# Cross-attention: division of the values' product in place of the probabilities, and one expert unit in another place

## The chip, the cores and the metric

The kernel runs on one core of a Trainium2 chip. Its engines work through queues of their own and meet through semaphores: TensorE (PE; its weight loads are shown as PEld), VectorE (DVE), ScalarE (ACT), GpSimd (POOL) and SyncE (SP), which issues most of the DMAs. The metric is device time in microseconds (us) of one launch, as the median of several runs; lower is better. Times inside the kernel come from one execution that the hardware profiler took.

## The reference, cut to what matters

A decoder block on 128 sequences of 64 tokens of 128 numbers: agent attention, cross-attention to a context of 64 tokens, and 16 experts of which each token uses two, each behind a layer norm and added to the input. The change is in the cross-attention, 16 heads of 8 numbers:

```python
Q = _split_heads(query @ Wq.T)
K = _split_heads(key @ Wk.T)
V = _split_heads(value @ Wv.T)
scores = jnp.einsum('bhqd,bhkd->bhqk', Q, K) / jnp.sqrt(jnp.float32(D_K))
causal = jnp.where(jnp.tril(jnp.ones((S, S), dtype=bool)), 0.0, NEG_INF).astype(scores.dtype)
scores = scores + causal[None, None, :, :]
attn = jax.nn.softmax(scores, axis=-1)
heads = jnp.einsum('bhqk,bhkd->bhqd', attn, V)
concat = heads.transpose(0, 2, 1, 3).reshape(B, S, D)
out = concat @ Wo.T
```

## The kernel before

The 128 sequences are worked on in eight groups of 16 (1024 tokens, eight tiles of 128). Every engine's program calls `both(e, g)` (run, L290): the experts of group e lie beside the two attentions of group g = e + 1. The first call has no e, the last no g, so there are seven full passes. The order of the work on each engine is written out by hand in its own `both`, and the engines wait for each other by semaphores.

Cross-attention of a group goes in four units u of four sequences, each with four planes q. On TensorE `scores(g, u)` (L587) adds the causal mask (L598) and the products of queries and keys (L606) in four PSUM banks of the ring "att", one bank a plane; the next unit's scores take the same banks and wait until they are read. On VectorE `maxima` (L1211) finds the largest score of each row; for planes 1 to 3 it subtracts it at once (L1222) and ScalarE takes the exponential of the whole plane (L935), for plane 0 ScalarE does both in eight short instructions, one a head (L930). `inverses` (L1225) sums the exponentials on VectorE (L1233) and takes the reciprocal (L1235); GpSimd multiplies 14 of the 16 planes of a group by it (L426), VectorE the other two (`normalise_x`, L1247). Then TensorE transposes the plane (`turn`, L624), ScalarE copies it out (`PT_moved`), `values` (L627) multiplies it with V, `project` (L640) with the output weights, and VectorE adds the result (`add_x`, L1239). For `values` the weights are V itself, spread over 32 columns with zeros (tile Vb), and the probabilities are moved, 128 columns at a time; for `project` the output weights were spread with zeros in a tile woM, by 16 DMAs at the start (L325). `values` of unit u runs two units behind its scores; the last two units' values and projections of group e fall in the next pass, among the first steps of group g: transposes of context and input, the values of the context (`values_of`, L654), the layer norm `norm`/`apply` (L1058, L1074), the pooled queries (L1286) and the products `moments` (L669).

An expert unit (`unit`, L520) is six products of 512 columns (`up`), one that spreads the routing weight (`weight`), and the down products of the unit before (`down_to`). VectorE's `hidden` (L1146) multiplies its parts, `result` (L1175) adds the sum of nine units. There are 18 units, 0 to 17, for each group. Unit 17 stands ahead of scores(0), its down products right behind them.

## Time and profile before

| | before |
|---|---|
| runs, us | 1148.42, 1150.33, 1150.6; median 1150.33 |
| span of the profiled execution, us | 1150.6 |
| busy: TensorE, its weight loads | 975.8 us (85%), 767.2 us (67%) |
| busy: VectorE, ScalarE, GpSimd | 788.8 us (69%), 577.3 us (50%), 227.7 us (20%) |
| chain that ended last, by engine | PE 62%, DVE 21%, ACT 10%, POOL 3% |

The profiled execution's span is that of its run, 1150.6 us; the runs differ by 2.2 us. Busy shares are means over stages with different limits, so the rows below are from single stages. The granted clock is a share of TensorE's full speed: 1.00 is 2.4 GHz, 0.50 is 1.2 GHz; a mean between them is a mixture. A row's name of a tile is the program's: banks are PSUM, M holds the transposed planes (pT), KQ and PXUT the planes themselves, Vb and woM the spread values and weights.

### The profile page before, as it was taken

The page shows a single profiled execution, that of the slowest core. Times are in us where ns is not written, and L with a number is a line of the kernel's source. Part 1 is how long each engine was busy: PE and PEld are TensorE (multiplying, and loading weights), DVE is VectorE, ACT ScalarE, POOL GpSimd, SP SyncE. Part 2 cuts the span into 40 slices and gives each one's busy share as a digit, 9 for nine tenths or more (in the row PEclk, how much of TensorE's full clock was granted, in tenths as well). Part 3 has the DMA queues.
Part 4 walks back from the last instruction along what each step waited for, and adds up shares of the span by engine and source line. Part 5 has one row for each costly group of instructions (what it writes and reads, how often), then busy time and mean ns, then how long its engine had stood idle before and what let it go on. Part 6 is the DMA issues. An engine that isn't in the chain of part 4 may idle for free.

```text
span 1150.6 us, 22137 instructions
## 1 busy us (share of the span) xinstructions
PE 975.8 (85%) x9069; PEld 767.2 (67%) x9069; DVE 788.8 (69%) x1841; ACT 577.3 (50%) x1148; POOL 227.7 (20%) x220
## 2 busy tenths in 40 slices
PE   6656899969998799978999699987999689987687
PEld 5553688737785587846886487855787477864566
DVE  3256866687866967678667878678666867669444
ACT  4434755367534665357553565346652575445322
POOL 6001410035000520024100440014200341004100
PEclk9886999979998899979999799989999799997789
DMA  5300010000100010000100010000100000000000
GB/s 146 80 1 1 2 38 1 11 10 2 38 10 10 2 38 1 11 10 2 37 11 1 11 31 8 10 11 2 38 1 10 11 2 1 10 11 1 1 1 19
DMA packets 28902, 18.36 MB, mean 16 GB/s; under 512 B 7649, under 2 KB 27394, under 8 KB 28802
## 3 DMA queue, kind: packets, MB, share of 16 engines
q1 hardware_dynamic: 26914, 12.48, 4.2%
q0 software_dynamic: 1280, 4.20, 1.2%
q8 instruction: 72, 1.18, 0.4%
q10 hardware_dynamic: 608, 0.27, 0.1%
q14 instruction: 28, 0.23, 0.1%
HBM read 12.62 MB, written 4.19 MB: 15 GB/s over the span
## 4 chain that ended last, share of the span: by engine, by line
PE 62%; DVE 21%; ACT 10%; POOL 3%; issue 3%; SPq 1%; DMA 0%; DVEq 0%; POOLq 0%
PE banks L510 7%; PE banks L674 5%; PE banks L491 5%; PE banks L493 5%; PE banks L492 5%; PE banks L606 4%; PE banks L624 4%; ACT M L867 3%; PE banks L648 3%; DVE PXUT L1222 3%; DVE mx L1221 3%; PE banks L769 3%; PE banks L541 2%; DVE sil L1166 2%; PE banks L598 2%
## 5 line engine op out<-in xcount | busy, mean ns | idle before, releaser
L874 ACT ACTIVATE sil<-banks,b 128x512 f32<-128x512 f32 x144 | 99.5, 691 | 199.6 <-PE banks L493 197.2
L867 ACT COPY M<-banks 128x512 f32<-128x512 f32 x208 | 122.9, 609 | 90.3 <-PE banks L624 70.2
L1166 DVE SCALAR_TENSOR_TENSOR sil<-banks,b,sil 128x512 f32<-128x512 f32 x128 | 95.8, 749 | 93.6 <-ACT sil L874 91.8
L510 PEld LDWEIGHTS banks<-w,hT 128*128 128x128 f32 x1152 | 151.5, 194 | 12.5 <-issue 7.2
L510 PE MATMUL banks<-w,hT 128*128 128x128 f32 x1152 | 154.5, 277 | 1.4 <-DVE hT L1173 1.4
L389 POOL DMA_DIRECT2D out_x<-xn x16 | 12.9, 809 | 534.3 <-DVE xn L1179 534.3
L426 POOL TENSOR_TENSOR PXUT<-PXUT,rx 128x512 f32<-128x512 f32 x80 | 87.2, 1117 | 101.7 <-DVE rx L1235 101.7
L1173 DVE TENSOR_TENSOR hT<-sil,banks 128x512 f32<-128x512 f32 x128 | 87.9, 687 | 25.1 <-PE banks L500 21.3
L624 PE MATMUL banks<-ident,PXUT 128*128 128x128 f32 x384 | 61.9, 301 | 31.7 <-ACT M L867 28.2
L598 PE MATMUL banks<-maskb,pick 32*64 32x512 bf16 x512 | 46.4, 506 | 46.6 <-ACT PXUT L930 28.2
L674 PEld LDWEIGHTS banks<-pooled,A 128*128 128x128 f32 x512 | 66.1, 207 | 19.9 <-DVE pooled L1286 18.6
L624 PEld LDWEIGHTS banks<-ident,PXUT 128*128 128x128 f32 x384 | 44.1, 150 | 52.6 <-ACT M L867 40.0
L674 PE MATMUL banks<-pooled,A 128*128 128x128 f32 x512 | 68.9, 293 | 12.0 <-DVE pooled L1286 12.0
L491 PE MATMUL banks<-xnT3l,w1h 128*128 128x512 f32 x144 | 75.1, 522 | 0.3 <-ACT sil L874 0.3
L491 PE MATMUL banks<-xnT3l,w3h 128*128 128x512 f32 x144 | 61.4, 427 | 11.1 <-DVE sil L1166 10.3
L1221 DVE TENSOR_REDUCE mx<-banks 128x8 f32<-128x512 f32 x96 | 65.3, 681 | 0.0
L867 ACT COPY PXUT<-banks 128x512 f32<-128x512 f32 x64 | 36.0, 588 | 54.6 <-PE banks L581 30.7
L606 PE MATMUL banks<-KQ 32*64 32x256 f32 x1024 | 60.9, 547 | 0.0
L493 PE MATMUL banks<-xnT3h,w1h 128*128 128x512 f32 x144 | 59.3, 412 | 0.0
L493 PE MATMUL banks<-xnT3h,w3h 128*128 128x512 f32 x144 | 59.2, 411 | 0.0
L1233 DVE TENSOR_REDUCE lx<-PXUT 128x8 f32<-128x512 f32 x96 | 59.2, 658 | 0.0
L492 PE MATMUL banks<-xnT3h,w1l 128*128 128x512 f32 x144 | 59.2, 411 | 0.0
(199 smaller groups left out, 2067.2 us busy)
## 6 DMA issues: line engine op xcount, KB each, us to landing
xin<-in_x SPq DMA_DIRECT2D x8, 512.0 KB, 4.1
cin<-in_ctx SPq DMA_DIRECT2D x8, 512.0 KB, 5.3
out_x<-xn POOLq DMA_DIRECT2D x16, 256.0 KB, 2.8
KQ<-in_L_attn_Wqkv SPq DMA_DIRECT2D x3, 512.0 KB, 5.3
KQ<-in_L_ffn_We SPq DMA_DIRECT2D x2, 512.0 KB, 4.6
KQ<-in_L_attn_Wo SPq DMA_DIRECT2D x1, 512.0 KB, 8.0
w<-in_L_ffn_We SPq DMA_DIRECT2D x1, 512.0 KB
woM<-xwT SPq DMA_DIRECT2D x16, 8.0 KB, 1.8
```

Source lines behind the costliest of these rows:

```text
L491: mm(ps(name)[:], wh[:, 2 * p:2 * p + 2, :], xl, start=True, stop=False)
L492: mm(ps(name)[:], wl[:, 2 * p:2 * p + 2, :], xh, start=False, stop=False)
L493: mm(ps(name)[:], wh[:, 2 * p:2 * p + 2, :], xh, start=False, stop=True).then_inc(fulled(name), 1)
L510: mm(ps(name)[:, P * t:P * t + P], hT[:, k % 2, P * t:P * t + P], w2[:, pair[k], :], start=(n == 0 and t == 0), stop=False, skip_group_che ...
L606: last = mm(ps(name)[64 * r:64 * r + 64, 256 * t:256 * t + 256], Qx[rr, S * b:S * b + S], Kx[rr, :, S * b:S * b + S], start=False, stop=Tr ...
L624: last = turn_over(ps(name)[:, P * j:P * j + P], src[:, P * j:P * j + P], ident[:])
L674: last = mm(ps(f"M_{n}")[:, P * k:P * k + P], A[:, 4 * (n % 4) + k, :], pooled[:], start=True, stop=True)
L867: cp(dst, ps(name)[:] if src is None else src).then_inc(ready, 1)
L874: nc.scalar.activation(sil[:, k % 2, :], ps(f"H1_{k}")[:], ACT.Silu, bias=b1[:, pair[k]:pair[k] + 1]).then_inc(sil_ready, 1)
L1166: V.scalar_tensor_tensor(sil[:, k % 2, :], ps(f"H3_{k}")[:], b3[:, p:p + 1], sil[:, k % 2, :], ALU.add, ALU.mult).then_inc(hid_ready, 1)
L1173: V.tensor_tensor(hT[:, k % 2, :], sil[:, k % 2, :], ps(f"C_{k}")[:], ALU.mult).then_inc(hT_ready, 1)
L1221: link(V.tensor_reduce(mx[:, q], sv, AX, ALU.max), g)
```

## The change

V gets a column of ones for each head (tile Vx in place of Vb). `values` now takes the transposed exponentials as weights and moves Vx, 18 columns for two heads at a time; what comes out has the tokens as rows, and beside each head's eight numbers the sum of its exponentials. The sums, reciprocals and multiplications of the planes go, and so do GpSimd's part of the cross-attention, woM and its 16 DMAs with the waits for them. `normalise_O` on VectorE divides the product instead. Then TensorE transposes it (`turn_O`), ScalarE copies it, and `project` multiplies it with the output weights as they are; the transposed product and the projection share one PSUM bank in turn. Plane 0 is subtracted on VectorE like the other three. Unit 17 now stands behind scores(0), its down products behind scores(1); the transposes and products that make the queries stand one unit earlier, and values_of(g, 3) ahead of the input's transposes.

```diff
-             "yx": ([f"Yx_{u}" for u in range(UX)], 1)}
+             "yx": ([f"{kind}_{u}" for u in range(UX) for kind in ("OT", "Yx")], 1)}
...
-            sp.wait_ge(consts, 3)
-            sp.wait_ge(setup_cp, 2)
-            for s in range(2):
-                for b in range(2):
-                    for gq in range(4):
-                        sp.dma_start(woM[32 * gq + 16 * b:32 * gq + 16 * b + 16, s, b, :],
-                                     xwT[32 * gq + 16 * s:32 * gq + 16 * s + 16, 3, :]).then_inc(spread_wo, 16)
...
-            nc.gpsimd.memset(woM[:], 0.0)
-            nc.gpsimd.memset(Vb[:], 0.0)
+            step(nc.gpsimd.memset(Vx[:], 0.0))
+            for r in range(2):
+                step(nc.gpsimd.memset(Vx[64 * r:64 * r + 64, :, :, (XC + 1) * r + XC:(XC + 1) * r + XC + 1], 1.0))
...
-                        nc.gpsimd.tensor_tensor(p, p, rx[:, u % 2, q].unsqueeze(2).to_broadcast([P, HALF, S]),
-                                                ALU.mult).then_inc(pn_ready, 1)
...
-                for j in range(4):
-                    for q in range(XQ):
-                        rr = slice(32 * q, 32 * q + 32)
-                        last = mm(ps(name)[rr, P * j:P * j + P],
-                                  Vb[:, 2 * u + j // 2, 2 * q + j % 2, :, :].rearrange("p a c -> p (a c)"),
-                                  pT[:, (XQ * u + q) % PT, j, :], start=True, stop=True, tile_position=(0, 32 * q))
+                w = 2 * (XC + 1)
+                for t in range(2):
+                    for j in range(XH // 2):
+                        for r in range(2):
+                            o0 = w * (XH // 2) * t + w * j
+                            last = mm(ps(name)[64 * r:64 * r + 64, o0:o0 + w],
+                                      pT[:, (XQ * u + j // 2) % PT, 2 * t + j % 2, 64 * r:64 * r + 64],
+                                      Vx[:, 4 * u + 2 * t + r, j, :], start=True, stop=True)
...
+            def turn_O(g, u):
...
+                pe.wait_ge(On_ready, UX * g + u + 1)
                 for t in range(2):
+                    last = turn_over(ps(name)[:, P * t:P * t + P], On[:, u % 2, t, :], ident[:])
...
+                for t in range(2):
+                    last = mm(ps(name)[:, P * t:P * t + P], OnT[:, u % 2, t, :], xwT[:, 3, :], start=True, stop=True)
...
-                unit(e, 17)
...
                     scores(g, 0)
-                if e is not None:
+                unit(e, 17)
+                if g is None:
                     down_to(e, 17)
...
                             scores(g, u + 1)
+                        if u == 0 and e is not None:
+                            down_to(e, 17)
+                        if u >= 3:
+                            turn_O(g, u - 3)
+                        if u >= 2:
+                            values(g, u - 2)
                         if u >= 3:
                             project(g, u - 3)
-                        if u >= 2:
-                            values(g, u - 2)
...
+            def normalise_O(g, u):
...
+                link(V.reciprocal(rx[:], ov[:, :, XC]))
+                V.tensor_tensor(On[:, u % 2].rearrange("p t (h c) -> p (t h) c", c=XC), ov[:, :, 0:XC],
+                                rx[:].unsqueeze(2).to_broadcast([P, 2 * XH, XC]), ALU.mult).then_inc(On_ready, 1)
...
-                    inverses(e, UX - 1, "e")
-                    normalise_x(e)
+                    normalise_O(e, UX - 3)
+                    add_x(e, UX - 4)
                     add_x(e, UX - 3)
                     for u in range(UX - 2):
                         stats_e(e, u)
+                    normalise_O(e, UX - 2)
...
                     add_x(e, UX - 2)
                     stats_e(e, UX - 2)
+                    normalise_O(e, UX - 1)
                 if g is not None:
                     apply("a", xin, xn, rstd_ready, 2 * g + 1, xn_ready)
...
                         maxima(g, u)
                         if u == 0:
+                            hidden(e, 17)
                             result(e, 1)
-                        else:
-                            if u == UX - 1:
-                                add_x(g, 0)
-                            inverses(g, u - 1)
+                        if u == UX - 1:
+                            normalise_O(g, 0)
```

TensorE's row at the first two scores of a full pass before (L598 and L606 are the scores, L500 the routing weight of unit 17, L510 down products, L516 the last of them):

```order
L500 MATMUL banks<-combsT,spread 128x512
L510 MATMUL banks<-w,hT 128x128 x4
L598 MATMUL banks<-maskb,pick 64x512 x16
L606 MATMUL banks<-KQ 64x256 x16
L510 MATMUL banks<-w,hT 128x128 x4
L516 MATMUL banks<-b2x,combT 128x128 x4
L598 MATMUL banks<-maskb,pick 64x512 x16
L606 MATMUL banks<-KQ 64x256 x16
```

Now, from behind scores(0) on (L468 to L470 are the six products of unit 17, L477 its routing weight, L487 and L493 down products, L575 and L583 the second scores):

```order
L468 MATMUL banks<-xnT3l,w1h 128x512
L469 MATMUL banks<-xnT3h,w1l 128x512
L470 MATMUL banks<-xnT3h,w1h 128x512
L468 MATMUL banks<-xnT3l,w3h 128x512
L469 MATMUL banks<-xnT3h,w3l 128x512
L470 MATMUL banks<-xnT3h,w3h 128x512
L477 MATMUL banks<-combsT,spread 128x512
L487 MATMUL banks<-w,hT 128x128 x4
L575 MATMUL banks<-maskb,pick 64x512 x16
L583 MATMUL banks<-KQ 64x256 x16
L487 MATMUL banks<-w,hT 128x128 x4
L493 MATMUL banks<-b2x,combT 128x128 x4
```

Unit 17 has moved behind the first scores, and the last down products behind the second.

VectorE's row at the same place before (L1221 and L1222 are a plane's maximum and subtraction, L1219 plane 0's maximum, L1179 result(1)):

```order
L1221 TENSOR_REDUCE mx<-banks 128x8
L1222 TENSOR_TENSOR PXUT<-banks,mx 128x512
L1179 TENSOR_TENSOR xn<-xe,banks 128x512
L1219 TENSOR_REDUCE mx<-banks 128x8
L1221 TENSOR_REDUCE mx<-banks 128x8
L1222 TENSOR_TENSOR PXUT<-banks,mx 128x512
```

Now (L1204 and L1205 are maximum and subtraction, L1153 and L1160 the two steps of hidden(17), L1166 result(1)):

```order
L1204 TENSOR_REDUCE mx<-banks 128x8
L1205 TENSOR_TENSOR PXUT<-banks,mx 128x512
L1153 SCALAR_TENSOR_TENSOR sil<-banks,b,sil 128x512
L1160 TENSOR_TENSOR hT<-sil,banks 128x512
L1166 TENSOR_TENSOR xn<-xe,banks 128x512
L1204 TENSOR_REDUCE mx<-banks 128x8
L1205 TENSOR_TENSOR PXUT<-banks,mx 128x512
```

hidden(17) and result(1) both stand between the first and the second maxima, and plane 0 has a subtraction.

TensorE's row behind the fourth scores before (L635 values, L624 the planes' transposes, L648 projection, L469 the context's transposes, L660 values of the context):

```order
L635 MATMUL banks<-M,Vb 32x128 x16
L624 MATMUL banks<-ident,PXUT 128x128 x16
L648 MATMUL banks<-woM,KQ 64x128 x8
L635 MATMUL banks<-M,Vb 32x128 x16
L469 MATMUL banks<-ident,cin 128x128 x8
L624 MATMUL banks<-ident,KQ 128x128 x8
L648 MATMUL banks<-woM,KQ 64x128 x8
L624 MATMUL banks<-ident,KQ 128x128 x8
L660 MATMUL banks<-xwT,ctxT 64x64 x8
L635 MATMUL banks<-M,Vb 32x128 x16
```

Now (L611 values, L598 the planes' transposes, L622 turn_O, L631 projection, L446 and L642 the context's):

```order
L611 MATMUL banks<-Vx,M 64x18 x32
L598 MATMUL banks<-ident,PXUT 128x128 x16
L622 MATMUL banks<-ident,KQ 128x128 x2
L611 MATMUL banks<-Vx,M 64x18 x32
L631 MATMUL banks<-xwT,KQ 128x128 x2
L446 MATMUL banks<-ident,cin 128x128 x8
L598 MATMUL banks<-ident,KQ 128x128 x8
L622 MATMUL banks<-ident,KQ 128x128 x2
L598 MATMUL banks<-ident,KQ 128x128 x8
L631 MATMUL banks<-xwT,KQ 128x128 x2
L642 MATMUL banks<-xwT,ctxT 64x64 x8
L611 MATMUL banks<-Vx,M 64x18 x32
```

The values are 32 products of 18 columns, and a transpose stands ahead of each shorter projection.

## Rows read from the trace of the kernel before

**Rows 1.** Stages: us, busy (count) PE, PEld, DVE, ACT, POOL; clock, DMA

```profile
499.60:514.00 14.40, 9.25 (x109) 4.63 (x109) 12.23 (x21) 7.61 (x24) 4.83 (x5) 0.63 0.06 18
...
527.00:542.67 15.67, 14.03 (x218) 10.88 (x217) 14.20 (x51) 10.32 (x22) 8.32 (x7) 1.00 0.01 3
...
547.82:551.24 3.42, 3.04 (x28) 2.85 (x27) 0.56 (x2) 1.76 (x4) 3.05 (x3) 1.00 0.00 0
...
551.24:554.65 3.41, 3.41 (x13) 2.83 (x12) 2.80 (x11) 2.87 (x4) 1.76 (x1) 0.50 0.06 19
```

**Rows 2.** Timeline, first two scores: start, length, engine, line, out<-in [idle before <-releaser]

```profile
486.39 0.48 PE L491 MATMUL banks<-xnT3l,w1h 128*128 128x512 f32 x1
...
489.00 1.88 PE L803 MATMUL banks<-xnT,xwT 128*128 128x512 f32 x4
...
493.32 0.64 PE L598 MATMUL banks<-maskb,pick 32*64 32x512 bf16 x16
...
494.75 1.16 PE L510 MATMUL banks<-w,hT 128*128 128x128 f32 x8
...
494.90 0.69 DVE L1219 TENSOR_REDUCE mx<-banks 128x8 f32<-128x512 f32 x1 [1.02 <-PE banks L606]
...
495.51 0.68 DVE L1221 TENSOR_REDUCE mx<-banks 128x8 f32<-128x512 f32 x1
...
496.83 0.68 DVE L1221 TENSOR_REDUCE mx<-banks 128x8 f32<-128x512 f32 x1
...
499.61 0.70 PE L598 MATMUL banks<-maskb,pick 32*64 32x512 bf16 x13 [0.93 <-DVE PXUT L1222]
...
502.05 0.69 DVE L1219 TENSOR_REDUCE mx<-banks 128x8 f32<-128x512 f32 x1 [1.90 <-PE banks L606]
```

**Rows 3.** Timeline from the fourth scores to the next moments

```profile
517.12 0.69 DVE L1219 TENSOR_REDUCE mx<-banks 128x8 f32<-128x512 f32 x1
...
526.88 0.63 PE L624 MATMUL banks<-ident,KQ 128*128 128x128 f32 x4 [0.69 <-POOL KQ L426]
...
528.76 1.09 PE L648 MATMUL banks<-woM,KQ 128*64 128x128 f32 x16 [0.25 <-ACT KQ L867]
...
536.61 1.08 PE L635 MATMUL banks<-M,Vb 128*32 128x128 f32 x32
...
537.24 2.14 DVE L1080 TENSOR_SCALAR xn<-xin,norm_a 128x128 f32<-128x128 f32 x8
...
542.67 3.84 PE L674 MATMUL banks<-pooled,A 128*128 128x128 f32 x32 [0.40 <-DVE pooled L1286]
...
548.65 1.96 PE L720 MATMUL banks<-gwT,xnT 128*128 128x16 f32 x16 [0.38 <-ACT xnT L867]
```

**Rows 4.** Groups by form: line, operation, count | busy us, mean ns | idle before

```profile
L904 ACT COPY Vb<-banks 64x256 f32<-64x256 f32 x64 | 23.5, 367 | 7.7 <-PE banks L660 7.2
...
L1235 DVE RECIPROCAL rx<-lx 128x16 f32<-128x16 f32 x64 | 16.2, 253 | 2.2
```

**Rows 5.** Timeline of the start, up to the first moments

```profile
16.79 0.32 SPq L319 DMA_DIRECT2D b2x<-in_L_ffn_bs  x1
...
20.71 10.67 SPq L325 DMA_DIRECT2D woM<-xwT  x16
...
30.71 1.62 PE L660 MATMUL banks<-xwT,ctxT 128*64 128x64 f32 x48 [0.78 <-ACT ctxT L867]
...
31.42 0.59 SPq L329 DMA_DIRECT2D KQ<-in_L_ffn_We  x1
...
33.75 1.07 ACT L867 COPY xnT<-banks 128x512 f32<-128x512 f32 x2
...
38.80 0.76 DVE L1277 CAST w1h<-KQ 128x1152 fp32r<-128x1152 f32 x1 [11.49 <-DMA KQ<-in_L_ffn_ws]
...
42.94 1.21 DVE L1286 TENSOR_REDUCE pooled<-xnT 128x128 f32<-128x1024 f32 x1
...
44.20 9.92 PE L674 MATMUL banks<-pooled,A 128*128 128x128 f32 x64 [9.19 <-DVE pooled L1286]
```

More of the change, by code:

```diff
@@ L37, in decoder_block @@
     UX = T // 2
-    BY_DVE = (XQ * UX - 4, XQ * UX - 3)
-    BY_POOL = [k for k in range(XQ * UX) if k not in BY_DVE]
+    XS = XQ * UX
     E, EG, EI = 16, 4, 64
@@ L177, in decoder_block @@
         pT = M[:].rearrange("p a b h -> p (a b h)").rearrange("p (k j q) -> p k j q", k=PT, q=P)
-        On = KQ[:, 7, :].rearrange("p (a q) -> p a q", a=2)
+        On, OnT = [KQ[:, 7, 512 * k:512 * k + 512].rearrange("p (a t d) -> p a t d", a=2, d=D) for k in range(2)]
         g1 = sb("g1", [P, T])
@@ L642, in project @@
                 wait_free(pe, g, name)
[L643 removed]
+                pe.wait_ge(OT_ready, UX * g + u + 1)
                 for t in range(2):
[L645 to L649 removed]
+                    last = mm(ps(name)[:, P * t:P * t + P], OnT[:, u % 2, t, :], xwT[:, 3, :], start=True, stop=True)
                 last.then_inc(fulled(name), 1)
@@ L684, in both @@
                     turn(e, UX - 2, (0, 1))
+                    turn_O(e, UX - 3)
+                    turn(e, UX - 2, (2, 3))
                     project(e, UX - 3)
[L686 removed]
                 if g is not None:
@@ L699, in both @@
                     values_of(g, 2)
+                if e is not None:
+                    turn_O(e, UX - 1)
+                if g is not None:
+                    values_of(g, 3)
                 if e is not None:
@@ L791, in both @@
                         unit(e, k)
-                for k in range(11, 16):
+                for k in range(11, 15):
                     unit(e, k)
@@ L797, in both @@
                     four(g, "xnT2_1", xn, 1)
-                unit(e, 16)
+                unit(e, 15)
                 if g is not None:
@@ L942, in both @@
                     PT_moved(e, XQ * (UX - 2))
+                    PT_moved(e, XQ * (UX - 2) + 1)
                     O_moved(e, UX - 3)
-                    for q in range(1, XQ):
-                        PT_moved(e, XQ * (UX - 2) + q)
+                    PT_moved(e, XQ * (UX - 2) + 2)
+                    PT_moved(e, XQ * (UX - 2) + 3)
                 if g is not None:
@@ L1012, in both @@
                               ps(f"combT_{n}")[0:2 * E, :])
-                for k in range(10, 16):
+                for k in range(10, 15):
                     silu(e, k)
@@ L1048, in _, with link @@
             V.tensor_reduce(plane[:], planes[:], AX, ALU.add).then_inc(plane_ready, 1)
-            links = {"a": 0, "e": 0}
-            def link(ins, g, kind="a"):
-                links[kind] += 1
-                signal, per = (vec_a, LINKS_A) if kind == "a" else (vec_e, LINKS_E)
-                ins.then_inc(signal, 1)
-                dve.wait_ge(signal, per * g + links[kind])
+            links = [0]
+            def link(ins, *_):
+                links[0] += 1
+                ins.then_inc(vec_step, 1)
+                dve.wait_ge(vec_step, links[0])
             def norm(g, kind, src, var, first=0):
@@ L1332, in both @@
                         hidden(e, k)
-                for k in range(14, 18):
+                for k in range(14, 17):
                     hidden(e, k)
                 if g is None:
+                    hidden(e, 17)
                     result(e, 1)
```

124 lines of the change are left out of this document (41 added, 83 removed).

## The prediction

> **What bounds the kernel now.** I read the page first (the busy shares), then the stages of one full pass, then the timeline of the stage in which the change lies, and the start last. The page has TensorE busy 85% of the span, VectorE 69%, ScalarE 50%, GpSimd 20%; but the four scores of a group are no TensorE stage. There VectorE is busy 12.23 of 14.40 us, TensorE 9.25, and the granted clock is 0.63 on average, a mixture of full and half speed [rows 1]. What alternates is visible in [rows 2]: scores(0) start at 493.32, the first maximum at 494.90; the maxima and subtractions of the four planes follow each other every 1.32 us (495.51 to 496.83); only when VectorE has let go of the last bank do the second scores run (499.61), and the next maximum stands 2.44 us after that, at 502.05, where the first scores took 1.58. So the bound is VectorE, then TensorE at a low clock, then VectorE. Behind the fourth scores (517.12) TensorE and ScalarE alternate, up to the first moments of the next group at 542.67: 25.55 us [rows 3]. In that stretch GpSimd's division ends a wait of TensorE only briefly (0.69 us at 526.88). At the start one chain stands alone: 16 small copies hold the SP queue from 20.71 for 10.67 us, the expert weights are issued behind them at 31.42, VectorE has them at 38.80, and the first moments run at 44.20 [rows 5].
>
> The passes repeat. I work out one full pass and count seven of them; the last group's tail has fewer steps and is put at zero.
>
> **Part A, the start: -9 us, once.** The 16 copies and their two waits go. The last issue ahead of them ends at 16.79 + 0.32 = 17.1; from the first weight issue to VectorE's first split took 38.80 - 31.42 = 7.4 us, so the weights lie there at 24.5. What is late next is not the split (38.80 to 42.94, 4.1 us, in VectorE's gap) but xnT: the copies of xnT stood at 33.75 and end at 34.8; the fourth V, which now goes ahead of them on ScalarE with two copies of 0.367 us [rows 4], moves that to 35.6. pooled takes 42.94 to 44.20, so the moments begin at 36.9 instead of 44.20: -7.3. Their 64 instructions took 9.92 us, 155 ns each, after 9.19 us of idle TensorE; 32 of them take 3.84, 120 ns each, where it had been at work [rows 3, 5]. With a wait of some 2 us in place of 9 I expect most of that 2.2 back. So between -7.3 and -9.5; I take -9. GpSimd's other memsets change by a few tenths, beside this.
>
> **Part B, unit 17 between scores(0) and scores(1): +0.2 us per pass.** A unit takes TensorE 489.00 - 486.39 = 2.61 us [rows 2]. Scores(0) start that much earlier, at 490.71, and the first maximum stands at 492.29. The first plane is now subtracted by VectorE like the others, so the maxima take 4 x 1.32 = 5.3 us in place of 0.61 + 3 x 1.32 = 4.6, and the last bank is free at 497.6. TensorE fills the gap with unit 17. But VectorE's row has unit 17 and result(1) ahead of maxima(1), and result(1) needs the last down products, which stand behind scores(1) on TensorE. So maxima(1) waits for more than its scores: scores(1) at full clock until 497.6 + 1.5 = 499.1, sixteen down instructions (eight take 1.16 with their drain, two such groups about 2.0) until 501.1, result(1) 0.7: 501.8, where it was 502.05. Of 2.61 us, 0.25 are left. This is what the move costs: before, the last down products and result(1) ran beside the maxima, now the next maxima queue behind them.
>
> The next two rounds lose the sums and reciprocals on VectorE, but these ran while TensorE made the next scores, and gain a subtraction each. A round was (517.12 - 502.05) / 2 = 7.53 us [rows 2, 3]; now it is 5.3 + 2.44 = 7.75 if the scores run as scores(1) did, or 5.3 + 1.5 = 6.8 if as scores(0). Nothing in the change gives TensorE more to do in these rounds, so I take the slow value: maxima(3) start at 501.8 + 15.5 = 517.3, +0.2. At full clock they would start at 515.4 (-1.8). If scores(1) and the down products run at half, their 3.5 us become twice that, less the wait already there: 2.75 us later.
>
> **Part C, the values and behind: +0.95 us per pass.** Removed: VectorE's sums and reciprocals, GpSimd's 14 products, seven of the eight short exponentials of each first plane. Added per unit: 32 products of 64 x 18, in the trace two instructions and two loads each, so 64 in place of 32 that move 128 columns (1.08 us at 536.61); two transposes, one copy, and a product of 4 instructions in place of 16 (1.09 at 528.76) [rows 3]. The trace has no 18-column product. The nearest row by its weights is the making of V: 64-column weights, both halves of the output in turn, 48 instructions in 1.62 us, 34 ns each [rows 5]: 64 make 2.1 us. The other neighbour is the gate: 128-column weights, 16 columns moved, 16 instructions in 1.96 us, 122 ns each [rows 3]. Half of that for half the columns is 61 ns, 3.9 us for a unit, if the two halves of the array load one after the other; columns alone would give less than 1 us. I take 2.1, since V alternates its halves in the same way. The divisions on VectorE are a reciprocal of 32 elements (16 take 0.253 [rows 4], so below 0.51; I take 0.35) and one product of 256 (eight operations on 128 take 2.14 at 537.24 [rows 3], 0.27 each, so below 0.54; I take 0.4), with the link between them 0.85.
>
> From the start of maxima(3), call it T: values(0) until T+2.1, then four transposes with ScalarE's copies and exponentials alternating, about 0.5 us a step, until T+6.1; values(1) until T+8.4; projection, the context's transposes, and turn(2) at T+9.75. In the trace it stood at 526.88 - 517.12 = 9.76. So the sums, reciprocals and GpSimd's products, which were on that path, are replaced by longer values at the same length. Values(2) end near T+15, values(3) at T+20.4 (before: 537.69 - 517.12 = 20.6). Then normalise_O(3) 0.85 stands ahead of the layer norm's apply (2.14 at 537.24, which was hidden), then xnT's transposes, copies and pooled: T+26.5 in place of 25.55, +0.95.
>
> **Part D, the clock in that stretch: +2.7 us per pass.** Before, it stays at 1.00 from 527.00 to 542.67, while TensorE is fed with 128-column products [rows 1]. In the gate's stretch TensorE reads as busy 3.04 of 3.42 us, but half of its time are 16-column products; the next stretch is granted 0.50 [rows 1, 3]. The new values are of that kind: 64 instructions of 18 columns, and between them turns that wait for ScalarE. I expect the clock to fall once per tail, about when values(1) run. At least half of a stretch of 3.41 us is lost then, 1.7; at most values, projection and context transposes twice as long, 2.1 + 0.5 + 1.0 = 3.6. I take 2.7, the middle. This is the term I know least; it may be 0.
>
> The Trainium skill's page "TensorE: Matmul & The Clock Gate", section "LDWEIGHTS (loading the stationary operand)", states a load as columns / 1.2 ns, which speaks against this change: 53 ns for 64 columns. The gate's 122 ns agree with its 107 for 128; V's 34 ns do not, unless two halves load at once. By the page's figure alone a unit's values would take an estimated 3.4 us, not 2.1.
>
> **Sum.** -9 + 7 x (0.2 + 0.95 + 2.7) = +18 us on the profiled 1150.6, which is 0.3 above the median of the runs (1150.33): 1168.
>
> **Rivals.** (1) The clock stays at 1.00 in the tail, as it does now: -9 + 7 x 1.15 = -1, 1149. For it: today's tail has waits of TensorE too. Against it: the gate. (2) Not slower, but faster: the scores run at full clock as well, since unit 17 keeps TensorE at work until the banks are free. With both later rounds at full, -9 + 7 x (-1.8 + 0.95) = -15, 1136; with one of them 1142. It decides where both rounds take 6.8 us and the tail stays at 1.00; with a fall in the tail the two cancel. Against it: from the end of the down products to the end of maxima(1) TensorE has 6 us with three masks. (3) The clock falls in the gap before scores(1), and result(1) holds VectorE at half speed: 2.75 per pass more, 1187. For it: TensorE's gap (from 494.8, when unit 17 is through, to 497.6) is as long as the present one (from 496.8, two down groups behind 494.75, to 499.61), and the present one ends in the low clock. (4) Loads of the two halves go one after the other: 1.3 us x 4 x 7 = 36 us more than (1): 1186, without any fall. Against it: V.
>
> **Chances.** Forecast 0.39 (1155 to 1178), rival 1 0.14, rival 2 0.24, rival 3 with more of the tail at half 0.18, rival 4 0.05. The range 1141 to 1192 leaves out the lower half of rival 2 and what adds rivals 3 and 4 up. A measurement here can tell 0.2%, 2.3 us: faster 0.25, same 0.11, slower 0.64.
>
> **What would show it.** Right: the first moments near 37 us; an idle VectorE of about 2 us ahead of result(1) and maxima(1) behind it at the old place; values at about 2.1 us; a granted clock below 1.00 between the fourth scores and the moments. Wrong: values near 1 or near 3.5 us; a tail at 1.00 throughout; rounds of the scores under 7 us; a start that another wait holds.

## The result, and the profile after

The changed kernel takes 1182.88 us (median of four runs, 1182.73 to 1186.28) against 1150.46 for the kernel before beside it: ratio 1.0292, 95% interval 1.0266 to 1.0319. It is slower by 32 us; 1168 was forecast, in a range of 1141 to 1192. One of the four launches of the kernel with the shorter tail, further below, took 1442.28 us at a mean granted clock of 0.631, and that kernel's time is the median of the other three.

The profiled execution has a span of 1184.6 us, 34.0 more than the one of before. A launch takes 1.7 us longer than its span (here 1186.28 us), in every run that lists both; so the span of 1150.6 us of before belongs to a launch near 1152.3 (an estimate), and not to the one of 1150.6. The starts of the first maximum of a group divide the 34.0 us: -7.0 up to the first group (89.40 in place of 96.40), +33.0 over the seven passes (963.7 in place of 930.7), +8.0 behind the last group's first maximum. In the table a round runs from a group's first, second or third maxima to the next, each by its start, and the pooled queries count from the end of their sum on VectorE.

| between, in one pass, us | before | after |
|---|---|---|
| pooled queries to first maximum | 85.3 | 81.8 |
| first to second maxima | 7.15 | 9.55 |
| second to third | 7.53 | 8.24 |
| third to fourth | 7.54 | 6.97 |
| fourth maxima to pooled queries (the tail) | 25.5 | 30.55 |
| whole pass | 133.0 | 137.1 |

Four of the seven passes look like this. The first has three rounds of 8.25, and two lose 1.4 and 2.7 us more to a clock that is low in other stretches too, one of them in its first round, which takes 11.16. The page of the changed kernel, busy time of the engines and the chain that ended last by engine:

```profile
PE 1010.9 (85%) x9773; PEld 813.6 (69%) x9773; DVE 731.3 (62%) x1729; ACT 540.1 (46%) x924; POOL 108.8 (9%) x109
...
PE 55%; DVE 34%; ACT 7%; issue 3%; DMA 1%; POOL 0%; ACTq 0%; DVEq 0%
```

VectorE, ScalarE and GpSimd all work less than before (by 57, 37 and 119 us), and the kernel is slower: VectorE's part of the chain rose from 21% to 34%. The page alone doesn't say where. The timeline of the changed kernel's first rounds does (start, length, engine, line, operation, idle time before it and what ended that), beside [rows 2]:

```profile
507.82 1.23 PE L583 MATMUL banks<-KQ 32*64 32x256 f32 x32
...
509.98 1.06 PE L493 MATMUL banks<-b2x,combT 128*128 128x128 f32 x8
...
511.08 0.69 DVE L1166 TENSOR_TENSOR xn<-xe,banks 128x512 f32<-128x512 f32 x1 [2.19 <-PE banks L493]
...
511.68 0.68 DVE L1204 TENSOR_REDUCE mx<-banks 128x8 f32<-128x512 f32 x1
...
513.24 0.37 PE L575 MATMUL banks<-maskb,pick 32*64 32x512 bf16 x1 [2.20 <-DVE PXUT L1205]
...
517.55 2.33 PE L583 MATMUL banks<-KQ 32*64 32x256 f32 x32
```

scores(1) (L583) are through at 509.05, but VectorE waits 2.19 us for the last down products (L493), does result(1), and only then the second maxima. TensorE in turn waits 2.20 us for its banks, and the next scores take 2.33 us where scores(1) took 1.23. The same pass by stages (busy time of PE, PEld, DVE, ACT, POOL; granted clock; DMA): three rounds, and the tail in two pieces, which answer to [rows 1]:

```profile
502.13:511.68 9.55, 7.06 (x79) 4.93 (x79) 7.19 (x11) 4.38 (x6) 0.00 (x0) 1.00 0.01 2
511.68:519.92 8.24, 4.44 (x49) 1.68 (x50) 5.24 (x9) 2.52 (x4) 0.79 (x1) 0.61 0.10 32
519.92:526.89 6.97, 4.78 (x68) 2.93 (x68) 5.25 (x8) 4.53 (x8) 0.00 (x0) 0.97 0.02 4
526.89:533.99 7.10, 5.12 (x99) 4.24 (x100) 5.94 (x10) 4.50 (x9) 0.00 (x0) 1.00 0.00 0
533.99:540.70 6.71, 6.71 (x73) 6.67 (x70) 1.20 (x3) 1.40 (x3) 0.00 (x0) 0.50 0.01 2
```

The clock is a mixture in the second round, and half for 6.71 us of the tail, while TensorE reads as busy all the time. The tail's timeline, beside [rows 3]:

```profile
526.78 2.05 PE L611 MATMUL banks<-Vx,M 128*64 128x18 f32 x64
...
532.58 0.42 DVE L1214 TENSOR_TENSOR KQ<-banks,rx 128x256 f32<-128x256 f32 x1
533.15 0.41 PE L622 MATMUL banks<-ident,KQ 128*128 128x128 f32 x2 [1.40 <-DVE KQ L1214]
533.49 3.23 PE L611 MATMUL banks<-Vx,M 128*64 128x18 f32 x64
...
537.67 1.91 PE L446 MATMUL banks<-ident,cin 128*128 128x128 f32 x8
...
549.40 2.05 PE L611 MATMUL banks<-Vx,M 128*64 128x18 f32 x64
...
552.23 2.14 DVE L1067 TENSOR_SCALAR xn<-xin,norm_a 128x128 f32<-128x128 f32 x8
...
554.42 1.09 PE L446 MATMUL banks<-ident,xn 128*128 128x128 f32 x8 [0.30 <-DVE xn L1067]
...
557.50 1.72 PE L656 MATMUL banks<-pooled,A 128*128 128x128 f32 x13 [1.12 <-DVE pooled L1259]
```

### The profile page after: what moved, and what is told of

The parts are those of the page before. It is cut to its first block, busy times and chain, and to the rows that moved or that the text cites. A ratio compares the mean times of both kernels' runs of the same rounds, so it can differ in the third digit from the quotient of the medians.

```text
span 1184.6 us, 23112 instructions
## 1 busy us (share of the span) xinstructions
PE 1010.9 (85%) x9773; PEld 813.6 (69%) x9773; DVE 731.3 (62%) x1729; ACT 540.1 (46%) x924; POOL 108.8 (9%) x109
## 3 DMA queue, kind: packets, MB, share of 16 engines
q8 instruction: 78, 1.28, 0.5%
## 4 chain that ended last, share of the span: by engine, by line
PE 55%; DVE 34%; ACT 7%; issue 3%; DMA 1%; POOL 0%; ACTq 0%; DVEq 0%
PE banks L487 7%; DVE mx L1204 7%; DVE PXUT L1205 5%; PE banks L611 5%; PE banks L468 4%; PE banks L583 3%; PE banks L470 3%; PE banks L469 3%; PE banks L656 3%; DVE sil L1153 3%; PE banks L598 2%; PE banks L756 2%; PE banks L446 2%; DVE xn L1067 2%; PE banks L575 2%
## 5 line engine op out<-in xcount | busy, mean ns | idle before, releaser
L487 PEld LDWEIGHTS banks<-w,hT 128*128 128x128 f32 x1152 | 153.0, 195 | 13.0 <-DVE hT L1160 5.3
L487 PE MATMUL banks<-w,hT 128*128 128x128 f32 x1152 | 156.2, 279 | 1.4 <-DVE hT L1160 1.4
L1153 DVE SCALAR_TENSOR_TENSOR sil<-banks,b,sil 128x512 f32<-128x512 f32 x128 | 95.7, 747 | 79.2 <-ACT sil L865 77.1
L1204 DVE TENSOR_REDUCE mx<-banks 128x8 f32<-128x512 f32 x128 | 87.3, 682 | 55.3 <-PE banks L583 55.3
L575 PE MATMUL banks<-maskb,pick 32*64 32x512 bf16 x512 | 51.6, 455 | 64.6 <-DVE PXUT L1205 53.3
L1160 DVE TENSOR_TENSOR hT<-sil,banks 128x512 f32<-128x512 f32 x128 | 87.8, 686 | 25.6 <-PE banks L477 21.7
L920 ACT ACTIVATE PXUT<-PXUT 128x512 f32<-128x512 f32 x96 | 60.2, 634 | 68.8 <-DVE PXUT L1205 68.1
L611 PEld LDWEIGHTS banks<-Vx,M 128*64 128x64 f32 x2048 | 74.5, 159 | 7.7 <-issue 6.7
L611 PE MATMUL banks<-Vx,M 128*64 128x18 f32 x2048 | 77.3, 226 | 0.9 <-ACT M L858 0.9
L575 PEld LDWEIGHTS banks<-maskb,pick 32*64 32x64 bf16 x512 | 12.0, 110 | 91.8 <-DVE PXUT L1205 51.3
L656 PEld LDWEIGHTS banks<-pooled,A 128*128 128x128 f32 x512 | 61.6, 196 | 17.1 <-DVE pooled L1259 16.5
L656 PE MATMUL banks<-pooled,A 128*128 128x128 f32 x512 | 64.9, 282 | 9.9 <-DVE pooled L1259 9.9
L468 PE MATMUL banks<-xnT3l,w1h 128*128 128x512 f32 x144 | 73.0, 507 | 0.3 <-ACT sil L865 0.3
L598 PE MATMUL banks<-ident,PXUT 128*128 128x128 f32 x384 | 63.0, 310 | 9.3 <-ACT M L858 9.3
L468 PE MATMUL banks<-xnT3l,w3h 128*128 128x512 f32 x144 | 59.7, 415 | 12.0 <-DVE sil L1153 11.2
L1205 DVE TENSOR_TENSOR PXUT<-banks,mx 128x512 f32<-128x512 f32 x96 | 66.3, 691 | 3.3
L598 PEld LDWEIGHTS banks<-ident,PXUT 128*128 128x128 f32 x384 | 46.9, 156 | 26.0 <-ACT M L858 18.9
L477 PE MATMUL banks<-combsT,spread 128*128 128x512 bf16 x128 | 50.2, 392 | 9.6 <-ACT combsT L858 9.6
```

What stands on the lines that cost most here:

```text
L468: mm(ps(name)[:], wh[:, 2 * p:2 * p + 2, :], xl, start=True, stop=False)
L487: mm(ps(name)[:, P * t:P * t + P], hT[:, k % 2, P * t:P * t + P], w2[:, pair[k], :], start=(n == 0 and t == 0), stop=False, skip_group_che ...
L575: mm(ps(name)[64 * r:64 * r + 64, :], pick[rr, a, :], maskb[rr, a].rearrange("p h s -> p (h s)"), start=(a == 0), stop=False, skip_group_c ...
L598: last = turn_over(ps(name)[:, P * j:P * j + P], src[:, P * j:P * j + P], ident[:])
L611: last = mm(ps(name)[64 * r:64 * r + 64, o0:o0 + w], pT[:, (XQ * u + j // 2) % PT, 2 * t + j % 2, 64 * r:64 * r + 64], Vx[:, 4 * u + 2 * t ...
L656: last = mm(ps(f"M_{n}")[:, P * k:P * k + P], A[:, 4 * (n % 4) + k, :], pooled[:], start=True, stop=True)
```

## The experiments

**The parts apart.** Two kernels, each with one half of the change. In the first the moved unit goes back:

```diff
-                for k in range(11, 15):
+                for k in range(11, 16):
...
+                unit(e, 17)
...
                     scores(g, 0)
-                unit(e, 17)
-                if g is None:
+                if e is not None:
                     down_to(e, 17)
```

> The changed kernel with unit 17, its down products, its hidden step and the queries' transposes back at their old places; the division stays behind the values. By the prediction the move costs 0.2 us a pass (scores(0) 2.6 us earlier, 2.4 of that given back ahead of maxima(1)), so this kernel is 1.4 us faster than the changed one: about 1181.5. Rival: the move is a gain. In the changed kernel's trace the moments reach the first maximum 3.5 us sooner, and the first round is 9.55 in place of 7.15; with four subtractions and no wait for result(1) that round should be about 7.8, so undoing loses 2.6 to 3.5 and gives back 1.75: 1189 to 1195. The first round decides: near 7.8 with the first maximum 85 us behind the pooled queries.

1191.05 us, ratio to before 1.0354 (1.0311 to 1.0398): 8 us slower than the changed kernel by the medians, and in the rival's range. Its four runs lie between 1185.13 and 1195.42 and the two intervals still overlap, so the size is less certain than the side. Per pass the pooled queries reach the first maximum in 84.3 us in place of 81.8, and the first round is 6.97 or 8.27, by the clock. The second kernel has the move alone, on the kernel before:

> The kernel before with the move alone (unit 17 behind scores(0), down products behind scores(1), hidden and result(1) behind the first maxima); division, woM and its copies as before. By the prediction the move is worth next to nothing, +0.2 a pass: 1152. Rival: scores(0) come 2.6 to 3.5 us earlier and only some of it is lost ahead of maxima(1): 1 to 2 us a pass are gained, 1136 to 1143. If the later rounds stay at 7.5 us the clock in them has nothing to do with the move.

1150.96 us, ratio 0.9982 (0.995 to 1.0014): the same, as predicted, though its ten runs spread from 1137.7 to 1153.47 and the profiled one, 1153.42, is among the slowest. The first maximum comes 2.5 us sooner (82.8), and the first round is 8.83 (granted clock 1.00) or, in every other pass, 10.4 (0.84). So on the old division the move brings what it promises and gives it back in the next round. The longer first round is in both kernels that have the move; next, the wait on result(1) alone was taken out of the changed kernel:

```diff
                         if u == 0:
                             hidden(e, 17)
+                        if u == 1:
                             result(e, 1)
```

> The changed kernel with result(1) behind the second maxima in place of ahead of them on VectorE. Theory (the prediction's part B): maxima(1) waited for result(1), 2.19 us idle and 0.6 of work; without it the first round is about 6.8 to 7.2 in place of 9.55, the later rounds as they are: 2.4 to 2.8 us a pass, 17 to 20 us in all: 1163 to 1166. Rival: the gap of TensorE ahead of scores(2) decides, and result(1) now stands where VectorE should free banks for it; the second round grows by 0.6 and the gain is 2 us a pass: 1169. Second rival: the clock falls somewhere else, earlier, and scores(1) run at half: gain below 1 us a pass, above 1176.

1154.56 us, ratio 1.005 (1.0031 to 1.0068): 28 us less than the changed kernel, by one line on VectorE, and more than any theory gave. Rounds one and two of a usual pass of this kernel, by stages, and VectorE's row in them:

```profile
626.91:633.88 6.97, 5.12 (x64) 3.18 (x65) 6.59 (x10) 4.38 (x6) 0.00 (x0) 1.00 0.00 0
633.88:640.85 6.97, 4.59 (x65) 2.97 (x66) 5.84 (x9) 2.52 (x4) 0.69 (x1) 1.00 0.01 2
```

```profile
633.88 0.69 DVE L1204 TENSOR_REDUCE mx<-banks 128x8 f32<-128x512 f32 x1 [0.21 <-PE banks L583]
...
639.18 0.68 DVE L1166 TENSOR_TENSOR xn<-xe,banks 128x512 f32<-128x512 f32 x1
640.85 0.69 DVE L1204 TENSOR_REDUCE mx<-banks 128x8 f32<-128x512 f32 x1 [0.99 <-PE banks L583]
```

The second maxima wait 0.21 us, and result(1) lies in a gap that was there anyway. The first round lost 2.58 us, and the second 1.28 although result(1) now stands in it: its clock is 1.00 where it was 0.61. The wait was paid twice, once as such and once as the idle time of TensorE behind which the clock fell.

**The start.** On the kernel before, the expert weights are issued first:

```diff
+            sp.wait_ge(setup_cp, 4)
+            for w_sb, we, ws in ((w1, We1, ws1), (w3, We3, ws3)):
+                sp.dma_start(w_sb[:, 0:E, :], we.rearrange("e d i -> d e i")).then_inc(loaded_e, 16)
...
             sp.wait_ge(consts, 3)
             sp.wait_ge(setup_cp, 2)
...
-            sp.wait_ge(setup_cp, 4)
-            for w_sb, we, ws in ((w1, We1, ws1), (w3, We3, ws3)):
...
```

> The kernel before with one edit: the four loads of the expert weights are issued ahead of the 16 copies into woM. Theory: the copies held the queue, so the first moments come 7 us sooner, as in the changed kernel's trace (38.8 in place of 44.2, first maximum 7.0 sooner): 1143.5. Rival: the start of the changed kernel came from what it saved elsewhere too (no copies competing for the DMA engines, GpSimd's clears): the first moments come only 3 to 5 us sooner, 1145.5 to 1147.5.

1142.37 us, ratio 0.9912 (0.9877 to 0.9946): 8.3 us less, as one queue's order predicts. Its timeline, SP's queue and the first moments, beside [rows 5]:

```profile
21.69 10.96 SPq L329 DMA_DIRECT2D woM<-xwT  x16
...
36.10 7.41 PE L674 MATMUL banks<-pooled,A 128*128 128x128 f32 x64 [1.11 <-DVE pooled L1286]
```

The 16 copies cost as much as ever, behind everything that waits.

**The tail.** From here on the base is the kernel with result(1) moved. Two things hold TensorE up in its tail: normalise_O(0) behind the fourth plane on VectorE, and ScalarE's copies, which alternate with exponentials. In the first kernel both go:

```diff
                 for q in range(XQ):
+                    if u == UX - 1 and q == 2:
+                        normalise_O(g, 0)
...
-                        if u == UX - 1:
-                            normalise_O(g, 0)
...
+                        if u == UX - 1:
+                            for q in range(XQ):
+                                PT_moved(g, XQ * (u - 2) + q)
                         for q in range(XQ):
-                            if u >= 2:
+                            if u == 2:
                                 PT_moved(g, XQ * (u - 2) + q)
```

> The kernel with result(1) behind the second maxima, and beside it two moves in the tail: normalise_O(0) between the second and the third plane of the last maxima (it stood behind the fourth), and on ScalarE the four copies of the transposed planes of unit 1 ahead of the last four exponentials (they alternated). No work is added or left out. TensorE's wait of 1.2 us ahead of the first turn_O goes, and values(1) start some 1.3 us sooner. Theory of the prediction's part D (the narrow products of the values let the clock fall, not the wait): the clock still falls about at values(1); the tail, from the last maxima to the pooled queries, is 29.2 in place of 30.5: 9 us less than the same kernel without the moves, 1145. Rival: the wait lets it fall: the granted clock stays at 1.00 in the tail, 26 to 27 us, 1120 to 1128.

1135.40 us, ratio 0.9872 (0.9824 to 0.9919), between the 1145 of the one theory and the 1120 to 1128 of the other. The tail is 26.4 us in four of seven passes and 27.9, 29.2 and 32.2 in the rest; and the profiled execution is the fastest of the three, 1129.74. In the second, normalise_O(0) alone is moved (the diff's lines on normalise_O):

> Base: result(1) behind the second maxima (1154.6, tail 30.5 at a clock that falls at values(1)). Here normalise_O(0) alone is moved between the second and third plane; ScalarE still alternates copies and exponentials, so TensorE's wait of 1.2 us goes from ahead of turn_O(0) to ahead of values(1), whose copies come at the old time. Theory now (idle TensorE ahead of values(1) lets the clock fall, wherever in that stretch it idles): the tail stays at 30 to 30.5, 1152 to 1155. Rival: the place of the wait matters, the clock stays in most passes: tail 27 to 28, 1130 to 1138.

1152.73 us, ratio 1.0022 (0.9995 to 1.0049): nothing gained, tail 30.25. The first row is where its wait went, the second the stage behind it; the third and fourth are the first two stages of 7 us of the tail with both moves:

```profile
653.87 2.37 PE L611 MATMUL banks<-Vx,M 128*64 128x18 f32 x48 [1.22 <-ACT M L858]
```

```profile
654.57:661.57 7.00, 7.00 (x71) 6.95 (x70) 1.20 (x3) 1.82 (x5) 0.00 (x0) 0.53 0.01 2
```

```profile
760.81:767.81 7.00, 6.21 (x146) 5.66 (x146) 5.93 (x10) 4.19 (x9) 0.00 (x0) 1.00 0.01 2
767.81:774.81 7.00, 6.58 (x118) 6.08 (x114) 2.40 (x8) 4.47 (x11) 0.00 (x0) 1.00 0.01 2
```

With the wait, in either place, the clock falls; without it, it stays at 1.00 in four passes of seven although the same narrow products run. So one unit's products alone need not do it. In the other three the clock is below 1.00 somewhere in the tail all the same; in two of them it was so already in the rounds ahead (0.72 to 0.75). Whether the narrow products matter at all, a pair of kernels on the base of the shorter tail is to tell: both add about 2 us to values(0) with the same 64-column weights, one 64 instructions that move 18 columns (1.96 us), the other 32 that move 128 (1.97).

```diff
-                for t in range(2):
+                for t in [0, 1] * (2 if u == 0 else 1):
```

> Base: the kernel with both moves in the tail (1136, tail 26.4 at 1.00 in its usual pass). Here values(0) are computed twice, with the same result: 64 more instructions of 18 columns a pass, 2.05 us more of TensorE's work without any wait; some of it takes the place of waits behind it. The prediction's theory (narrow products let the clock fall): it falls in the tail of most passes, tail 30 to 32, 1160 to 1175. Rival (only waits count): it stays at 1.00, tail 28.0 to 28.5, 1147 to 1151.

```diff
+                if u == 0:
+                    for j in range(XH // 2):
+                        for r in range(2):
+                            mm(ps(name)[64 * r:64 * r + 64, 320:320 + P],
+                               pT[:, (XQ * u + j // 2) % PT, j % 2, 64 * r:64 * r + 64], ident[:],
+                               start=True, stop=True)
```

> The partner of the run before: in place of the second values(0), 16 products with the same 64-column weights that move 128 columns of a constant into columns nobody reads, about 1.1 to 1.7 us more of TensorE's work. Theory of narrow products: the clock stays at 1.00 in the tail, 27.5 to 28, 1143 to 1147. If it falls here as often as in the run before, the columns moved aren't what decides; if in neither, only waits count.

1148.17 us, ratio 0.9983 (0.9963 to 1.0002), and 1143.91, ratio 0.9947 (0.9916 to 0.9978). The tail's first 7 us, the narrow kernel and then the wide one:

```profile
643.03:650.03 7.00, 7.00 (x143) 6.60 (x144) 5.67 (x10) 1.44 (x3) 0.00 (x0) 0.76 0.00 0
```

```profile
645.35:652.35 7.00, 6.21 (x120) 5.67 (x121) 5.83 (x10) 2.44 (x5) 0.00 (x0) 1.00 0.00 0
```

With the narrow ones the clock comes down in the tail of every pass (29.4 us, with no wait between the last scores and them); with the wide ones the tail is 28.1 us in six passes of seven and 29.6 in one. That is on the side of the prediction's theory. But the two kernels differ in the number of instructions and weight loads as well as in the columns moved, so which of these decides isn't shown. Nor did the theory get the time: about half of 7 us is spent at the lower level, less than expected, and 1148.17 lies in the rival's range, in part because the clock holds better elsewhere: the rounds of this kernel are at 6.97 in every group behind the first. In the wide kernel's rounds the clock falls more often (first round 7.4 to 7.8 us in five of the seven groups behind the first), which no theory here explains. A third kernel mixed eight wide transposes among the narrow products of each of two units:

> The kernel of the run before, and 8 transposes of a constant, 128 columns wide, among the 32 products of values(0) and of values(1) each, into columns of the bank that nobody reads: 1 us of TensorE's work more a unit at full clock, 2 a pass. Theory (columns moved): the clock stays at 1.00 through the tail although nothing else is changed: 3.3 us a pass given back, 2 paid; tail 27.5 to 28.5. Rival (the waits, or the weight loads, let it fall): it falls as before and the tail is 2 to 3 us longer than in the run before. If the run before has 1.00 already, this one only pays the 2 us: 14 us more.

1214.42 us, ratio 1.0575 (1.053 to 1.0619), against both theories: the tail is 37 to 39 us. Its tail by stages, and a piece of the timeline at full clock:

```profile
678.67:685.67 7.00, 7.00 (x79) 5.53 (x80) 4.05 (x7) 0.39 (x1) 0.00 (x0) 0.76 0.01 2
685.67:692.67 7.00, 6.66 (x52) 4.87 (x51) 1.98 (x3) 4.29 (x9) 0.00 (x0) 0.50 0.00 0
```

```profile
679.05 0.41 PE L613 MATMUL banks<-Vx,M 128*64 128x18 f32 x8
679.39 0.33 PE L612 MATMUL banks<-ident 128*128 128x128 f32 x1
679.65 0.41 PE L613 MATMUL banks<-Vx,M 128*64 128x18 f32 x8
```

From group to group it is 0.60 us, where eight such instructions alone take 0.25 (64 in 2.00): a transpose between products of another form costs 0.35 us. So it adds much time and little work. Why the clock falls here too and stays at half for some 17 us (682.3 to 699.4), with TensorE shown as busy for nearly all of it, stays open: the form and the columns were changed together.

**What is left in the rounds.** Three kernels ask what the best order of either division is worth. Plane 0 goes back to ScalarE, on the base of the shorter tail:

```diff
+                    if q == 0:
+                        V.tensor_reduce(mx[:, q], sv, AX, ALU.max, negate=True).then_inc(mx_ready, 1)
+                        continue
                     link(V.tensor_reduce(mx[:, q], sv, AX, ALU.max))
...
```

> The same base, with the first plane of each unit as before the change: ScalarE takes maximum and exponential in eight short instructions, VectorE subtracts three planes. The prediction's part B has the fourth subtraction at 0.7 us a round. Theory: rounds 6.3 in place of 6.97 where the clock is at 1.00, 3 or 4 rounds a pass: 2 to 2.6 us a pass, 1118 to 1122. Rival: ScalarE's eight instructions (1.77 us a unit) push the copies of the transposed planes, and the tail gives it back: 1130 to 1136. Second rival: with shorter rounds TensorE idles less and the odd passes with a low clock go as well: 1110 to 1116.

1117.01 us, ratio 0.9721 (0.9685 to 0.9757). The first round is 6.24, as worked out; the second and third stay at 7.2 to 7.5, with a clock below 1.00. So the rounds bring only 5 of the 14 us between the two profiles. The tail brings 12: it is 26.0 to 26.3 us in all seven passes, and the long ones are gone, as the second rival had it; 3 go the other way ahead of the first maxima. The kernel before, with its own division and three moves (weights first, unit 17, result(1) later):

> The kernel before with its division, and three moves: expert weights issued ahead of the copies into woM (8 us in its own run), unit 17 behind scores(0), result(1) behind the second maxima. With the move alone the first maximum stood 2.5 us sooner and the first round was 8.8 or 10.4 in place of 7.2. Theory: that excess is the wait on result(1) alone; without it the first round is 7.0 to 7.5, and 2.3 us a pass are kept: 1142.4 - 16 = 1126. Rival: before's sums and reciprocals hold the rounds, and result(1) lengthens the second by 0.6: 1131. Second rival: the clock falls in the first round in some passes (1.3 us each): 1130 to 1135.

1116.7 us, ratio 0.972 (0.9686 to 0.9754). That is 9 us below its theory's 1126, and the two divisions come out level once the waits around them are out of the way. Last, TensorE's two waits in the rounds of the kernel with plane 0 on ScalarE are filled:

```diff
+                        if u == 2 and e is not None:
+                            turn(g, 0, (0, 1, 2))
+                            idle_work(e, 10)
+                            turn(g, 0, (3,))
...
                             down_to(e, 17)
+                            idle_work(e, 20)
```

> Base: the kernel with the first plane on ScalarE again (1117.0; its second and third rounds are 7.2 to 7.5 us, with a clock that falls behind TensorE's two waits of some 2.8 and 1.5 us, where the first round takes 6.24). Here those two waits are filled with 20 and 10 transposes of a constant, 128 columns wide, all of one form, into a bank that nobody reads then; TensorE has nothing else to do in that time. Theory (idle TensorE in the rounds lets the clock fall): it stays at 1.00, the second and third rounds take 6.24 to 6.4: 2.2 us a pass, 1100 to 1105. Rival (the transposes count as little work, as those mixed with the values did): the clock falls all the same, and the transposes end behind the banks' release: 1117 to 1125. Second rival: the fall only moves into the tail, which grows by 1 to 3 us: 1112 to 1125.

1099.03 us, ratio 0.9548 (0.9523 to 0.9573), 4.5% faster than the kernel before. Its second round by stages, behind it the same round without the filling:

```profile
476.48:482.72 6.24, 5.99 (x85) 4.90 (x86) 5.15 (x8) 3.53 (x11) 0.69 (x1) 1.00 0.01 3
```

```profile
480.19:487.71 7.52, 5.55 (x65) 3.32 (x66) 5.14 (x8) 3.52 (x11) 0.79 (x1) 0.79 0.08 26
```

30 transposes a pass whose results nobody reads save 18 us. So it is TensorE's idle time in the rounds that lets the clock fall, and the fall that makes them long. The kernel with the old division has rounds of 8.07 and 7.40 at granted clocks of 0.79 and 0.77 too; it was not filled, so 1099 against 1117 says nothing of which division is better.

## Why the prediction was right, and where not

**The sign and the place were right, the size 15 us short.** One usual pass was put at +3.85 us and is +4.1, seven of them 28.7. That they agree so well is partly luck: part B came out 1.2 us lower, parts C and D together 1.4 higher. What was not in the sum: the last group, put at zero, is +8.0 (its first round alone is 11.15 us in place of 6.85), and the three passes that differ from the usual one add 4.3. The start gave 2 us less than its -9.

**Part A, -9: the step holds, 2 us short.** The profile of the changed kernel shows -7.0 at the first maximum, of which 5.4 are the earlier moments and 0.9 their shorter run (9.04 in place of 9.92):

```profile
30.59 1.10 PE L446 MATMUL banks<-ident,cin 128*128 128x128 f32 x8 [1.10 <-ACT Wvo L849]
...
36.45 1.07 ACT L858 COPY xnT<-banks 128x512 f32<-128x512 f32 x2
...
38.84 9.04 PE L656 MATMUL banks<-pooled,A 128*128 128x128 f32 x64 [2.04 <-DVE pooled L1259]
```

The context's transposes are here 1.8 us later than in the profile of before (the products of the setup ahead of them take 10.15 us in place of 8.73, at a granted clock of 1.00 in both; why stays open), so the moments stand at 38.84 and not at 36.9; in the kernel with the weights first they stand at 36.10 and take 7.41, so both terms of the -9 are there (-8.1 and -2.5, the first maximum 10.6 us sooner). The kernels without the copies reach the first maximum between 84.0 and 89.4 us: the start varies that much from one kernel's profile to the next.

**Part B, +0.2: right in its wait, wrong in what the clock does on either side of it.** The wait was worked out to 9.5 us from first to second maxima and is 9.55. Of the later rounds, 7.75 or 6.8 was forecast; it was 8.24 and 6.97, one of each kind. The gain ahead was larger than 2.61: 3.5, since the clock no longer falls behind the gate, as it did before [rows 1]: it is 1.00 from 562.0 to 572.2, where that stage lies now. With the unit at its old place 1.0 of it is still there in most passes, so that part doesn't come from the move. The net is -1.0 and not +0.2. Most of that is the gain ahead, 0.9 more than forecast. The two rounds together, 15.2 in place of 15.5, agree by luck: one value was taken for both, where each follows its own clock, one longer and one shorter. Rival 2 had them at 6.8 at full clock, "since unit 17 keeps TensorE at work"; what brought 6.97 was result(1) out of the way. The prediction saw the queue behind result(1) and priced it as a wait, but not what TensorE's idle time behind it does to the next round.

**Part C, +0.95: 1.7.** The values take 2.00 to 2.05 us at full clock, as taken from V (64 instructions, 31 ns each). The Trainium skill's page "TensorE: Matmul & The Clock Gate", section "LDWEIGHTS (loading the stationary operand)", would have given an estimated 3.4; the trace doesn't bear that out for halves loaded in turn, so rival 4 falls. (Its price of 1.3 us took the page's figure; the 3.9 us worked out from the gate's row would have made it 1.8 a unit, 50 us in all and 1199.) The moments stand 557.50 - 526.89 = 30.6 us behind the start of the fourth maxima; less 3.35, the price of the half-clock stretch (half of 6.71), that is 27.25, against 25.55 before. turn(2), 12.5 behind it, is at 9.8 without that price; 9.75 was forecast. The missing 0.75 lies mostly between values(2) and values(3), 6.06 us from start to start (543.34 to 549.40) where the forecast's times make 5.4: a turn_O and a projection that waits for its copy stand there in a row. One thing was overlooked: the transposes of unit 1 ended sooner than thought, and 1.40 us of idle TensorE stood ahead of turn_O(0), until normalise_O(0) was through behind the fourth plane.

**Part D, +2.7: 3.35, at the place named.** The clock falls when values(1) run. Its reason was half the story: with one unit's narrow products the clock fell in the usual pass only beside a wait of 1.2 to 1.4 us, which the prediction's "turns that wait for ScalarE" named without a price. Without the wait it fell in every tail only with twice the narrow products. Rival 1 (1.00 throughout) came true in the kernel with the shorter tail, in four passes of seven. Rival 3 fell in the usual pass: scores(1) ran at full clock, and the low clock came one round later. But in one of the seven passes, in the last group, and in every other pass of the kernel with the move alone, the clock fell as rival 3 said, in the first round, and result(1) kept VectorE waiting, in the changed kernel 3.79 us in place of 2.19. There it cost 1.6 us (11.16 in place of 9.55):

```profile
370.75 2.08 PE L487 MATMUL banks<-w,hT 128*128 128x128 f32 x8
372.62 1.51 PE L493 MATMUL banks<-b2x,combT 128*128 128x128 f32 x8
...
374.16 0.69 DVE L1166 TENSOR_TENSOR xn<-xe,banks 128x512 f32<-128x512 f32 x1 [3.79 <-PE banks L493]
```

## What to carry to other kernels

When work is moved between two steps of an alternation, follow what stands behind it on the other engine's queue: its wait costs once as time, and again if an engine that idles meanwhile comes back with a lower clock. Look at the granted clock stage by stage before and after, and where it is a mixture, try first to take out the idle time ahead of the fall, even with work that nobody needs. Judge a large edit only with the queue orders around it varied: here two different divisions came out level, and four small edits around the new one (result(1), normalise_O(0), ScalarE's copies, plane 0) decided 66 us.

## What the hardware showed that was not expected

- Work without use at the right place saves time: 30 transposes a pass, 3.6 us of TensorE's time, took 18 us off the kernel. Put among products of another form they cost 0.35 us each in place of 0.12, and the clock fell for longer than without them.
- A row that shows TensorE busy throughout does not show full speed: it read as busy 7.00 of 7.00 us in stretches granted 0.76 and 0.53. The granted clock has to be read beside it.
- In the changed kernel VectorE's first split of the weights takes 3.39 us while GpSimd adds; the second, of the same size and behind that addition, 1.36:

```profile
28.27 2.80 POOL L397 TENSOR_TENSOR xr<-xin,bo_b 128x1024 f32<-128x1024 f32 x1 [2.26 <-DVE xn L1067]
28.90 3.39 DVE L1252 TENSOR_TENSOR w1l<-KQ,w1h 128x1152 fp32r<-128x1152 f32 x1
...
32.99 1.36 DVE L1252 TENSOR_TENSOR w3l<-KQ,w3h 128x1152 fp32r<-128x1152 f32 x1
```

The kernel before and the one with the weights first settle it. They differ only in the order of SP's issues; in the first the addition and the split lie apart, in the second they overlap, and both take longer:

```profile
27.39 2.35 POOL L410 TENSOR_TENSOR xr<-xin,bo_b 128x1024 f32<-128x1024 f32 x1 [2.26 <-DVE xn L1080]
39.60 1.36 DVE L1279 TENSOR_TENSOR w1l<-KQ,w1h 128x1152 fp32r<-128x1152 f32 x1
```

```profile
27.31 2.80 POOL L410 TENSOR_TENSOR xr<-xin,bo_b 128x1024 f32<-128x1024 f32 x1 [2.26 <-DVE xn L1080]
27.94 3.39 DVE L1279 TENSOR_TENSOR w1l<-KQ,w1h 128x1152 fp32r<-128x1152 f32 x1
```

The Trainium skill's page "GPSIMD Engine Reference", section "Specifications", says that GpSimd shares its SBUF interfaces with VectorE, and that instructions with two SBUF inputs, as this one, contend; the trace agrees with it.
